# Two causal attentions on one core: the products with values in parts of 16, 16 and 8 matmuls, in slots apart, each waiting for its own units

## The reference

```
# the ratio attention
dot = einsum('bhid,bhjd->bhij', q, k)
vals = q_norm_sq + k_norm_sq.transpose(0, 1, 3, 2)
scores = dot * dot / (vals - 2.0 * dot + EPSILON)        # then a causal mask
out = einsum('bhij,bhjd->bhid', softmax(scores), v)

# the zeroed attention
att = einsum('bhqe,bhke->bhqk', q, k) / sqrt(he)
mask = tril(ones((c, c)), k=-1)
att = softmax(att * mask)                                # masked scores count as exp(0)
out = einsum('bhqk,bhke->bhqe', att, v)
```

## Time and profile before

| | |
|---|---|
| time, median of 3 runs | 2868.76 us (2867.21 to 2870.6) |
| profiled execution | 2875.2 us, its span 2873.5 us |
| mean granted clock of TensorE | 0.970 |
| PE busy | 2642.3 us, 92% |
| DVE, ACT, POOL busy | 79%, 72%, 63% |
| L197, ratio attention | 5120 records, 190.8 us |
| L197, zeroed attention | 5120 records, 182.5 us |
| ACT's exponential L1200, idle before it for L197 | 117.2 us, 63 times |
| POOL's L1430, busy | 227.3 us, 640 instructions |

### The profile page before, as it was taken

How to read it: one execution, slowest core, us unless ns; L and a number is a source line. 1 busy time by engine, 2 the same in 40 slices (tenths; PEclk the granted TensorE clock), 3 DMA queues, 4 the chain that set the end, 5 groups by cost and what they waited for, 6 DMA issues and landing times. The chain is left out here.

```text
span 2873.5 us, 75169 instructions
## 1 busy us (share of the span) xinstructions
PE 2642.3 (92%) x27002; PEld 1830.7 (64%) x27044; DVE 2283.8 (79%) x6931; ACT 2076.6 (72%) x3782; POOL 1814.5 (63%) x3152
## 2 busy tenths in 40 slices
PE   5999999999999999997799599999999999699999
PEld 3777777777777777773233366666666666466766
DVE  5999999999999999984655477777777777389988
ACT  4999898998999999993243266666666666478886
POOL 3766767667777667762511276666666666488885
PEclk8999999999999999998899699999999999799999
DMA  4434443334443343412000455564556454000001
GB/s 113 72 60 70 78 78 65 64 64 76 78 78 70 63 66 70 70 36 54 0 1 0 93 102 90 93 95 87 93 92 101 89 85 65 1 16 23 23 23 38
DMA packets 110387, 182.21 MB, mean 63 GB/s; under 512 B 27008, under 2 KB 96384, under 8 KB 97920
## 3 DMA queue, kind: packets, MB, share of 16 engines
q1 hardware_dynamic: 106560, 176.61, 34.0%
q10 hardware_dynamic: 3456, 0.79, 0.2%
HBM read 116.25 MB, written 60.29 MB: 61 GB/s over the span
## 5 line engine op out<-in xcount | busy, mean ns | idle before, releaser
L792 POOL TENSOR_TENSOR ratio_scores<-ratio_scores,ratio_max_cols 128x512 f32<-128x512 f32 (+3 forms) x1024 | 729.2, 729 | 318.8 <-DVE ratio_max_cols L702 316.5
L1312 DVE CUSTOM_DVE_ANT_0 zeroed_unused<-bank,zeroed_drop 128x512 bf16<-128x512 f32 (+3 forms) x1024 | 448.6, 486 | 175.0 <-PE bank L182 171.2
L182 PE MATMUL bank<-ratio_k_stack,ratio_q_stack 102*128 102x512 bf16 (+7 forms) x2048 | 508.1, 303 | 29.2 <-DVE ratio_max_cols L702 13.3
L1200 ACT ACTIVATE zeroed_prob<-bank 128x512 f32<-128x512 f32 x640 | 368.3, 592 | 218.3 <-PE bank L197 117.2
L702 DVE CUSTOM_DVE_ANT_0 ratio_scores<-bank,ratio_scores 128x512 f32<-128x512 f32 (+3 forms) x1024 | 472.4, 489 | 22.2
L564 ACT ACTIVATE ratio_prob<-bank 128x512 f32<-128x512 f32 x640 | 380.1, 594 | 105.6 <-PE bank L478 105.3
L692 DVE TENSOR_TENSOR ratio_scores<-bank,ratio_inverse 128x512 f32<-128x512 f32 x640 | 435.8, 681 | 16.9 <-PE bank L182 9.7
L475 PE MATMUL bank<-const_f_sb,ratio_scores 128*128 128x128 f32 x2560 | 409.9, 274 | 0.7 <-ACT ratio_prob L564 0.7
L553 ACT ACTIVATE ratio_inverse<-bank 128x512 f32<-128x512 f32 x640 | 382.6, 598 | 12.6 <-PE bank L185 12.5
L1430 POOL TENSOR_SCALAR_AFFINE_SELECT zeroed_prob<-zeroed_prob 128x256 f32<-128x256 f32 (+1 forms) x640 | 227.3, 362 | 247.8 <-ACT zeroed_prob L1200 246.6
L557 ACT ACTIVATE ratio_inverse<-ratio_inverse 128x1024 f32<-128x1024 f32 x320 | 338.6, 1058 | 10.1
(11 more groups left out here) (178 smaller groups left out, 5333.3 us busy)
## 6 DMA issues: line engine op xcount, KB each, us to landing
ratio_q_stack<-ratio_parts_q SPq DMA_DIRECT2D x186, 128.0 KB
ratio_k_stack<-ratio_parts_k SPq DMA_DIRECT2D x186, 128.0 KB
zeroed_q_stack<-zeroed_parts_q SPq DMA_DIRECT2D x186, 128.0 KB, 4.7
zeroed_k_stack<-zeroed_parts_k SPq DMA_DIRECT2D x186, 128.0 KB, 7.5
ratio_parts_q<-ratio_parts SPq DMA_DIRECT2D x96, 128.0 KB
ratio_parts_k<-ratio_parts SPq DMA_DIRECT2D x96, 128.0 KB
zeroed_parts_q<-zeroed_parts SPq DMA_DIRECT2D x96, 128.0 KB
zeroed_parts_k<-zeroed_parts SPq DMA_DIRECT2D x96, 128.0 KB
```

The lines of the kernel that those rows point to most:

```text
L182: i = e.matmul(bank[:, off:off + w], qs[0:rows, s, hh, ib * P:(ib + 1) * P], ks[0:rows, s, hh, 0:w], start=(k == 0), stop=mask is None, sk ...
L792: i = e.tensor_tensor(seg, seg, mx[:, pair % M_BUFS, c:c + 1].to_broadcast([P, w]), ALU.subtract)
L1200: e.activation(prob[:, n % FOLD_PROBS, 0:wd], exp_banks[n % 2][:, 0:wd], ACT.Exp, scale=0.25).then_inc(s["prob"])
L1312: i = e.tensor_tensor_reduce(unused[:, n % 2, at], bank[:, at], drop[:, L - (ib + 1) * P:L], 1.0, 0.0, ALU.add, ALU.max, mx[:, pair % FOLD ...
```

## The change

The parts become ((3,), (2, 0), (1,)): 16, 16 and 8 matmuls. Part 0 asks for 8 units of its group, part 1 for 9, part 2 for all 10. They stand at offsets 9, 11 and 12 in the ratio attention and 9, 11 and 13 in the zeroed one. The copy of the group's sums keeps its slot (offset 13), and all other work keeps its slot as well. `attended_by` is worked out from `ATTEND`, so a unit with blocks 2 and 0 is now given free by part 1 and one with blocks 1 by part 2. By slot number modulo 10, the parts of the ratio attention move from 6, 7, 8 to 5, 7, 8 and those of the zeroed attention from 9, 0, 1 to 7, 9, 1.

```diff
-ATTEND = ((3,), (2,), (1, 0))
+ATTEND, ATTEND_UNITS, ATTEND_AT = ((3,), (2, 0), (1,)), (8, 9, 10), (9, 11, 12)
+KEEP_GROUP_AT = 13
...
+def attend_at(n, slots, groups):
+    for part, at in enumerate(slots):
+        g, off = divmod(n - at, N_UNITS)
+        if off == 0 and 0 <= g < groups:
+            return g, part
+    return None, None
+
+def ratio_attend_at(n, groups):
+    return attend_at(n, [BACK_LAG + at for at in ATTEND_AT], groups)
...
# ratio attention, PE (ACT's keep_group goes by BACK_LAG + KEEP_GROUP_AT)
-                g, part = divmod(n - BACK_LAG - N_UNITS, N_UNITS)
-                if 0 <= g < total // N_UNITS and part < len(ATTEND):
-                    q.wait_ge(s["prob"], (g + 1) * N_UNITS)
+                g, part = ratio_attend_at(n, total // N_UNITS)
+                if g is not None:
+                    q.wait_ge(s["prob"], g * N_UNITS + ATTEND_UNITS[part])
...
-ATTEND_LAG = 11
+Z_ATTEND_AT = (9, 11, 13)
...
-GROUPS_FROM, ROW_STEPS = ZEROED_LAG + ATTEND_LAG + 7, (71, 81, 91, 101)
+GROUPS_FROM, ROW_STEPS = ZEROED_LAG + 18, (71, 81, 91, 101)
...
# zeroed attention, PE (keep_group and masked_part go with the last part)
-                g, part = divmod(n - ZEROED_LAG - ATTEND_LAG, N_UNITS)
-                if 0 <= g < total // N_UNITS and part < len(ATTEND):
-                    q.wait_ge(s["kept"], (g + 1) * N_UNITS)
+                g, part = attend_at(n, [ZEROED_LAG + at for at in Z_ATTEND_AT], total // N_UNITS)
+                if g is not None:
+                    q.wait_ge(s["kept"], g * N_UNITS + ATTEND_UNITS[part])
```

More of the change, by code:

```diff
@@ L636, in act @@
                     keep_row(b, step // 2)
-                g, part = divmod(n - BACK_LAG - N_UNITS, N_UNITS)
-                if 0 <= g < total // N_UNITS and part == len(ATTEND):
+                g, at = divmod(n - BACK_LAG - KEEP_GROUP_AT, N_UNITS)
+                if 0 <= g < total // N_UNITS and at == 0:
                     keep_group(g)
@@ L1269, in act @@
                     exponential(n - ZEROED_LAG)
-                g, part = divmod(n - ZEROED_LAG - ATTEND_LAG, N_UNITS)
-                if 0 <= g < total // N_UNITS and part == len(ATTEND) - 1:
+                g, part = attend_at(n, [ZEROED_LAG + at for at in Z_ATTEND_AT], total // N_UNITS)
+                if part == len(ATTEND) - 1:
                     keep_group(g)
```

## The result

| | before | changed |
|---|---|---|
| time, median of 5 runs | 2868.76 us (2863.21 to 2871.58) | 2797.78 us (2795.31 to 2800.76) |
| ratio, 95% interval | | 0.9745 [0.973, 0.9759] |
| span of the profiled execution | 2873.5 us | 2796.0 us |
| PE busy | 2642.3 us, 92% | 2615.3 us, 94% |

A forecast was written before the change was run, and what follows sets the result against it. Both attentions were taken as bound by PE and what PE waits for. The zeroed attention's -51 us and the ratio attention's -4 made -55, which off the median of 2868.76 gave 2814 us, range 2793 to 2853.

The forecast's parts named there:

- The parts' cost: PE time per part of the products with values: 1.11 us for 16 matmuls, 0.89 for 12, 0.68 estimated for 8.
- The steady row: Zeroed attention: four groups gain 1.58, 0.21, 1.10 and 0.41 us from filled waits, -3.30 us a row, -51 us over 15.5 rows.
- slots 2 to 6 give nothing back: Zeroed attention: slots 2 to 6 were taken not to grow by what slots 0 and 1 lose.
- the sum of 1.29: Zeroed attention, third group: PE's waits for DVE of 0.64, 0.24 and 0.41 us, inside which the 1.11 us part fits.
- ACT's bound: Zeroed attention: one exponential fewer queued behind the copy could win up to 0.5 us in two groups; taken as 0.
- I count that once in a row: Ratio attention: slot 5's 0.28 us wait for DVE, filled once per 40-slot row, gives -4 us; bounds 0 and -34.
- the second rival: Ratio attention: norms and parts no longer overlap, costing 9.6 us and losing the gain of 4; 2827 us, chance 15%.
- the drain has little to cover: End of the zeroed loop, given with the first rows as reason to count 15.5 of its 16 rows.
- the tail of 0.18: Zeroed attention, third group: 0.18 us that may go too, counted only in the range's low end.
- ACT's wait of 3.41 us: Zeroed attention, exponential of slot 1 waiting for the last part; the wait was to move to the copy of the sums.
- The first: Zeroed attention: only POOL's waits go, -16 us, DVE's shift, ratio attention unchanged; 2853 us, chance 12%.
- The third: Zeroed attention: slots 2 to 6 regain what slots 0 and 1 lose, up to 1.10 us a group; 2884 us, chance 7%.

The follow-up runs named there:

- z_last_15: Changed kernel with the zeroed attention's last part and ACT's copy of the sums in slot 3 instead of slot 1; ratio to the kernel before 0.9815.
- z_adjacent_early: Changed kernel with the zeroed attention's three parts in adjacent slots 7, 8 and 9; ratio to the kernel before 0.9824.
- r_only: Kernel before with the new parts and slots in the ratio attention only; ratio to the kernel before 1.0002.
- r_adjacent: Changed kernel with the ratio attention's parts in slots 6, 7, 8, mixing norms and first part again; ratio to the kernel before 0.9759.
- z_split_only: Kernel before with the zeroed attention's new split and own-unit waits, in the old slots 9, 0, 1; ratio to the kernel before 0.9919.
- phase_before_64: Kernel before with 64 extra matmuls ahead of the zeroed attention's first scores, moving instruction block borders; ratio to the kernel before 0.9995.
- z_only: Kernel before with the new parts, slots and waits in the zeroed attention only; 2804.1 us, ratio to the kernel before 0.9764.
- z_slots_only: Kernel before with the zeroed attention's old split (16, 12, 12) in new slots 7, 9, 1, own-unit waits; 2809.5 us, ratio to the kernel before 0.9787.
- z_copy_14: Changed kernel with ACT's copy of the zeroed attention's sums in slot 2 instead of slot 1, parts unmoved; ratio to the kernel before 0.9759.
- both phases: Changed kernel with 64 or 32 extra matmuls ahead of the zeroed attention's first scores, moving instruction block borders; ratios to the kernel before 0.9752 and 0.9758.

## Why the prediction was right, and where it was off

**The parts' cost.** 1.11 and 0.89 us were read, and 0.68 for the part of 8 was an estimate. The trace after has 0.57 to the next scores with 0.10 ahead, 0.67. Right.

**The steady row.** -3.17 against -3.30, and each group within 0.11 us of its term. The premise, that slots 2 to 6 give nothing back, held: slot 2 changed by 0.00 and slots 3 and 4 of every second group by -0.26 and 0.00. z_last_15 and z_adjacent_early show how narrow that is: with 0.67 us more taken out of slot 1, slot 3 gave it back in full in every second group. In the third group the sum of 1.29 leaves out the tail of 0.17 of its last wait. With it the waits are 1.46, the part fills 1.11 of them, and the 0.19 in the bracket above and its tail are what is left.

**ACT's bound.** One exponential less behind the copy was bounded at 0.5 us in two groups and taken at 0. The 0.26 us of slot 3 went, but 0.23 came back in slot 6. Zero was right as a sum.

**The ratio attention.** -4 was forecast, r_only shows 0 within 2 us. The step that failed is "I count that once in a row": in slots 35 and 36 the part did fill the wait (+0.42 and -1.11, 0.69 us less), and slot 39 gave it back (+0.67); slots 2 to 8 lost 0.32 and slots 25 to 32 gained 0.35. These are slots of a row of 40. No other engine's waits were followed there; the row as a whole stayed 78.9, and a wait filled in one slot came back in another.

**The norms.** Taken apart from the part they would have cost up to 9.6 us by the second rival. r_adjacent, which mixes them again, is not faster, so costing them at nothing was right. The Trainium skill ("TensorEngine Tiling (Array Packing)", "Key Properties") says that changing the tiling mode drains TensorE. One more such change a half is there and no run shows a cost of it in time; that waits for DVE cover it, as the prediction had it, is not shown.

**The miss of 16 us.** The step is "the drain has little to cover" and what the sum left out. Long rows (14.4 us) were in the trace of before as rows of 52 to 56 us, and the prediction does not name them; they belong to the parts in slots 9, 0, 1. Four traces with that placing (before, r_only, z_split_only, phase_before_64) have four or five such stalls of over 1.1 us each, eight with a part in slot 7 and own-unit waits (the changed kernel, z_only, z_slots_only, z_last_15, r_adjacent, z_copy_14 and both phases) have none. The runs with parts in 7, 8, 9 and with waits for all units have none at count 449 either. The drain gave 10.8, by a wait of 1.89 us for POOL and by less time at the half clock, and some 5 us of it come and go with that clock. With what lies ahead of the loop and behind the drain (3.1) that is 28 us beyond the sum. Six are missing from the sum's own terms (4 of the ratio attention, 2 at the ends of the loop), and 6 belong to the one profiled execution of before.

**The range.** That 2797.8 lies within it (from 2793) is partly luck. Its low end was made of ACT's 0.5 us in two groups and of the tail of 0.18, which gave nothing. The long rows and the drain, which gave the 16 us, were in no bound.

**The signs.** The waits of slots 8 and 9 went but for 0.19 us, and the norms stand alone, as foretold. ACT's wait of 3.41 us did not move to the copy: the copy runs without a wait, and the exponential waits 1.63 us for its own scores. PE's share is 97.5% from 1700 to 2370 us, not near 99%, and the ratio row is not 0.3 us shorter.

**What remains open.** Why a due block waits up to 10.3 us and more with the parts in 9, 0 and 1, and at most 8.0 us otherwise, is not shown. Adjacent parts two slots earlier stay at 8.0 us, so it isn't that three parts stand in a row. The waits for all ten units aren't it either: z_split_only waits for its own units and stalls. That a late fetch stops TensorE is shown by the count, which is the same with the borders moved by half a block. That the gathers hold the fetch back is read from the times; no run here changed the gathers.

**Rivals.** The first (only POOL's waits go) is what z_split_only is by construction, and its row gave the 1.06 us that it was priced by (22 us as a time), but that is not all that happened. The third failed for the changed kernel, but its mechanism is real, as z_last_15 and z_adjacent_early show.

None of the twelve runs was faster than the changed kernel.

## What to carry to other kernels

List the waits of the bounding engine slot by slot, and move work of the same engine into the slot where its wait stands; each group's gain can then be read off to 0.1 us. A slot that loses work must be followed by idle time of the engines that feed the next ones, or the loss comes back as a wait. A part may be moved forward only as far as its own data allow, so its wait has to be narrowed first: with the wide wait the same placing cost 235 us.

## What the runs showed of the hardware

TensorE's instructions arrive in blocks of 16 KB over a DMA queue of their own, 256 records each with the semaphore instructions, and a fetch takes 0.88 to 1.96 us. Under a burst of gathers (DMA share 1.06 to 1.08 from 1925 to 1935 us) the next block came 16.9 us after the last, and TensorE stood for 1.9 to 2.8 us each time that it had used up what was fetched, in 17 of 17 cases at the same count. The pause then costs more than itself, since the granted clock was 0.81 to 0.85 in the 10 us from 1935, the stall and what follows it:

```profile
1925.00:1930.00 5.00, 4.15 (x42) 2.81 (x39) 4.96 (x20) 4.01 (x10) 4.18 (x15) 1.00 1.06 129
1930.00:1935.00 5.00, 4.89 (x80) 3.51 (x81) 4.42 (x21) 2.14 (x5) 2.26 (x9) 1.00 1.08 132
1935.00:1940.00 5.00, 3.11 (x47) 2.30 (x46) 2.23 (x8) 3.72 (x8) 1.84 (x6) 0.85 0.04 5
1940.00:1945.00 5.00, 5.00 (x35) 2.99 (x34) 3.54 (x15) 3.39 (x8) 2.97 (x9) 0.81 0.23 63
```

(kernel before; the last three columns are the granted clock, the DMA share and GB/s.) A row of instructions that pauses "for issue" between two equal matmuls is the sign to look for, and the queue of instructions the place. Not every such stall has that mark: the first of before is put down to ACT's exponential (1.89 us), and the last of these ended at 1937.90, 0.86 us before TensorE went on.
